# A gated cross-attention block on one core: the maxima of a group of heads half a group further ahead

## What is computed

```
q = rms_norm(x @ w_q.T + b_q, g_q); k, v and k_img, v_img likewise from the context
img_x = softmax(q @ k_img.T * SCALE) @ v_img
txt_x = softmax(where(mask, q @ k.T * SCALE, -1e9)) @ v
out = (txt_x + img_x) @ w_o.T + b_o
x = x + tanh(g_xattn) * out
x = x + tanh(g_ffn) * ffn(layernorm(x))
```

## Time and profile before

| | |
|---|---|
| median of 3 runs | 3852.16 us (3851.76 to 3853.89) |
| the profiled execution: time | 3848.66 us |
| the profiled execution: span | 3846.9 us |
| TensorE busy | 3264.6 us (85%) |
| VectorE busy | 2226.5 us (58%) |
| ScalarE busy | 1561.6 us (41%) |
| GpSimd busy | 1199.9 us (31%) |
| granted TensorE clock, mean share | 0.902 |

### The profile page before, as it was taken

One profiled execution on the slowest core, in us unless ns is written; L12 is line 12 of the kernel. 1 busy time (PEld: TensorE's weight loads), 2 busy tenths in 40 slices (PEclk: granted clock), 3 DMA queues, 4 the chain that ended last, 5 costly groups with the idle time before them and its releaser, 6 DMA issues. The chain is left out here.

```text
span 3846.9 us, 51052 instructions
## 1 busy us (share of the span) xinstructions
PE 3264.6 (85%) x16256; PEld 1969.7 (51%) x16256; DVE 2226.5 (58%) x3716; ACT 1561.6 (41%) x2933; POOL 1199.9 (31%) x386
## 2 busy tenths in 40 slices
PE   6999999977999899999989999998985551799993
PEld 5777888753343443434344343434423440677773
DVE  5666666645565655656565565656535658433335
ACT  3444343322555555555555555555551110122222
POOL 0000000002575655657565565657560000000000
PEclk8999999986898998989899898989897875899997
DMA  5666667685324242333424243332204542101004
GB/s 148 168 167 166 165 168 167 165 120 123 79 59 94 48 93 56 85 75 65 91 50 94 50 91 70 71 87 54 59 6 137 162 155 87 69 23 44 22 22 175
DMA packets 395564, 367.89 MB, mean 96 GB/s; under 512 B 41392, under 2 KB 324080, under 8 KB 392824
## 3 DMA queue, kind: packets, MB, share of 16 engines
q1 hardware_dynamic: 352776, 331.99, 36.4%
q10 hardware_dynamic: 42624, 33.56, 2.7%
HBM read 227.54 MB, written 137.92 MB: 95 GB/s over the span
## 5 line engine op out<-in xcount | busy, mean ns | idle before, releaser
L874 ACT ACTIVATE at_probs<-at_st 128x512 f32<-128x512 f32 (+1 forms) x1664 | 944.6, 596 | 841.2 <-PE at_st L740 828.3
L902 DVE TENSOR_REDUCE at_cm<-at_mx 128x2 f32<-128x896 f32 x768 | 820.1, 1089 | 668.3 <-PE at_mx L756 667.5
L721 POOL TENSOR_TENSOR at_added<-at_added,at_probs 128x2048 f32<-128x2048 f32 x192 | 877.7, 4572 | 121.3 <-ACT at_probs L874 109.8
L756 PE MATMUL at_mx<-at_kst,at_qst 97*128 97x448 f32 (+1 forms) x2048 | 643.3, 368 | 158.9 <-DVE at_cm L902 115.0
L740 PE MATMUL at_st<-at_qst,at_kst 101*128 101x512 f32 (+1 forms) x1664 | 741.4, 461 | 12.6 <-ACT at_probs L874 12.2
L740 PEld LDWEIGHTS at_st<-at_qst,at_kst 101*128 101x128 f32 (+1 forms) x1664 | 314.1, 194 | 563.7 <-ACT at_probs L874 367.5
L756 PEld LDWEIGHTS at_mx<-at_kst,at_qst 97*128 97x128 f32 x2048 | 391.0, 194 | 287.2 <-DVE at_cm L902 196.2
L778 PE MATMUL at_acc<-at_probs,at_vt 128*32 128x512 f32 (+2 forms) x3584 | 529.8, 668 | 0.0
L721 POOL TENSOR_TENSOR at_added<-at_probs 128x2048 f32<-128x2048 f32 x32 | 146.0, 4562 | 705.8 <-ACT at_probs L874 705.8
L691 POOL MEMSET at_ones<- 128x32 f32 x1 | 0.1, 129 | 826.5 <-POOLq L262 826.5
L1309 ACT ACTIVATE ff_h<-ff_psa,ff_b1c,alpha 128x512 f32<-128x512 f32 x128 | 99.6, 779 | 378.2 <-PE ff_psa L1291 378.2
(11 more groups left out here) (190 smaller groups left out, 4789.3 us busy)
## 6 DMA issues: line engine op xcount, KB each, us to landing
at_kst<-k_high SPq DMA_DIRECT2D x256, 200.1 KB
at_kst<-k_low SPq DMA_DIRECT2D x128, 200.1 KB
pj_xin<-in_ctx_dram SPq DMA_DIRECT2D x96, 256.0 KB, 4.2
k_high<-pj_kh SPq DMA_DIRECT2D x96, 256.0 KB, 3.1
k_low<-pj_kl SPq DMA_DIRECT2D x96, 256.0 KB, 4.7
values<-pj_vs SPq DMA_DIRECT2D x96, 256.0 KB, 4.6
at_vt<-values SPq DMA_DIRECT2D x32, 768.0 KB
at_qst<-q_high SPq DMA_DIRECT2D x64, 256.0 KB, 4.2
```

The costliest lines, as they stand in the source:

```text
L721: pool.tensor_tensor(added[:], so_far, probs[:, SLOT[t]], ALU.add).then_inc(S["add_done"], 1)
L756: pe.matmul(mx[:, bank, 0:kn], qst[w.j][0:MROWS, h, qt * P:(qt + 1) * P], kst[w.j][0:MROWS, h, k0:k0 + kn], start=True, stop=True).then_in ...
L874: act.activation(probs[0:kn, SLOT[t], h, :], st[0:kn, h % 2, :], ACT.Exp, scale=SCALE).then_inc(S["exp_done"], 1)
L902: dve.tensor_reduce(dst, mx[:, 2 * slot:2 * slot + 2, 0:kn], AX.X, ALU.max).then_inc(S["mx_free"], 1)
```

## The change

The maxima of a group are issued in two parts. `EARLY` = 14 of the 32 pairs are issued two groups ahead, in tiles 8 to 12, and the other 18 one group ahead, in tiles 0 to 6. The tops stand in tile 7 (`TOPS`), behind heads 2 and 3. A tile has five places, one behind each of heads 0, 1 and 2 and two behind head 3, and `spread` deals the matmuls over them. Ahead of the first group 14 pairs of the second one are issued. GpSimd's join stands ahead of the third add (`JOIN_AT` = 2). VectorE's body has 18 reductions, the negation, the finish, and 14 reductions of the group after next. The sets of instructions are the same, and ScalarE's copies move with the tops.

```diff
--- before.py
+++ after.py
@@ -564,14 +564,13 @@
         self.G = 3 * i + j
         self.known = isinstance(i, int)
         self.first = self.known and self.G == 0
-        self.last = self.known and self.G == GROUPS - 1
 
     def at(self, step):
         j = self.j + step
         return Group(self.i + (j // 3), j % 3)
 
-    def below(self, n):
-        return self.known and self.G < n
+    def followed(self, step):
+        return not self.known or self.G + step < GROUPS
 
 
 def attend(nc, scratch, out_t, b_v, b_v_img):
@@ -593,7 +592,9 @@
     SUMS_LATE = {(0, 1): [4], (1, 1): [5, 6]}
     TEXT = [0, 1, 2, 3, 4, 7, 8, 9]
     NADD = len(TEXT) - 1
-    JOIN_AT = 4
+    JOIN_AT = 2
+    EARLY = 14
+    TOPS = 7
     RING = 5
     SLOT = [0, 1, 2, 3, 4, 0, 1, 2, 0, 1, 2, 3, 4]
     TRIPLES = GROUPS // 3
@@ -627,10 +628,16 @@
         NC = 2 + 1 + 6
 
         plan = {}
-        places = [(t, h) for t in range(KT) for h in (0, 1, 2, 3, 3, 3)]
-        for n in range(2 * NPAIR):
-            plan.setdefault(places[n], []).append((n // 2, n % 2))
-        top_at = {(11, 1): 0, (11, 3): 1}
+
+        def spread(tiles, heads, step, pairs):
+            places = [(t, h) for t in tiles for h in heads]
+            singles = [(step, m, r) for m in pairs for r in range(2)]
+            for n, single in enumerate(singles):
+                plan.setdefault(places[n * len(places) // len(singles)], []).append(single)
+
+        spread(range(TOPS), (0, 1, 2, 3, 3), 1, range(EARLY, NPAIR))
+        spread(range(TOPS + 1, KT), (0, 1, 2, 3, 3), 2, range(EARLY))
+        top_at = {(TOPS, 2): 0, (TOPS, 3): 1}
 
         def keys(t):
             return P if t < KT - 1 else KLAST
@@ -795,16 +802,15 @@
                 done.then_inc(S["s_done"], 1)
 
             def body(g):
-                w = None if g.last else g.at(1)
                 before = None if g.first else g.at(-1)
                 for t in range(KT):
                     for h in range(HG):
                         scores(g, t, h)
-                        if w:
-                            for m, r in plan.get((t, h), []):
-                                maxima(w, m, r)
-                            if (t, h) in top_at:
-                                tops(w, top_at[t, h])
+                        for step, m, r in plan.get((t, h), []):
+                            if g.followed(step):
+                                maxima(g.at(step), m, r)
+                        if (t, h) in top_at and g.followed(1):
+                            tops(g.at(1), top_at[t, h])
                         if h == 1:
                             if t > 0:
                                 values(g, t - 1)
@@ -824,6 +830,9 @@
                     maxima(Group(0, 0), m, r)
             for half in range(2):
                 tops(Group(0, 0), half)
+            for m in range(EARLY):
+                for r in range(2):
+                    maxima(Group(0, 1), m, r)
             groups(pe, body)
             g = Group(TRIPLES, GROUPS - 1 - 3 * TRIPLES)
             pe.wait_ge(S["exp_done"], NST * GROUPS)
@@ -872,7 +881,7 @@
                         if h == 0:
                             ring(g, t)
                         act.activation(probs[0:kn, SLOT[t], h, :], st[0:kn, h % 2, :], ACT.Exp, scale=SCALE).then_inc(S["exp_done"], 1)
-                        if not g.last and (t, h) in top_at:
+                        if g.followed(1) and (t, h) in top_at:
                             copy_top(g.at(1), top_at[t, h])
                         if before:
                             if (t, h) == (0, 0):
@@ -922,12 +931,15 @@
                 dve.tensor_tensor(res[:], part[:, 0, :], part[:, 1, :], ALU.mult).then_inc(S["res_done"], 1)
 
             def body(g):
-                if not g.last:
-                    for m in range(NPAIR):
+                if g.followed(1):
+                    for m in range(EARLY, NPAIR):
                         reduce(g.at(1), m)
                     negate(g.at(1))
                 if not g.first:
                     finish(g.at(-1))
+                if g.followed(2):
+                    for m in range(EARLY):
+                        reduce(g.at(2), m)
 
             dve.memset(neg[:], 1.0).then_inc(S["const_dve"], 1)
             dve.wait_ge(S["const_dve"], 1)
@@ -938,6 +950,8 @@
             for m in range(NPAIR):
                 reduce(Group(0, 0), m)
             negate(Group(0, 0))
+            for m in range(EARLY):
+                reduce(Group(0, 1), m)
             groups(dve, body)
             finish(Group(TRIPLES, GROUPS - 1 - 3 * TRIPLES))
 
```

## The result

| | before | after |
|---|---|---|
| median of 4 runs each | 3851.96 us (3850.92 to 3853.89) | 3981.68 us (3980.64 to 3982.85) |
| ratio, 95% interval | | 1.0336 (1.0318 to 1.0354) |
| profiled execution, its span | 3848.7, 3846.9 us | 3981.9, 3980.1 us |
| period of a group, mean of groups 1 to 29 | 61.5 us | 66.0 us |
| first score of group 0 | 920.12 us | 939.60 us |

The change makes the kernel slower by 3.4%, 130 us. The forecast was 4015 us with a range of 3885 to 4090: direction and mechanism held, and the forecast is 33 us too high.

What follows compares the result with a forecast made beforehand. TensorE was taken to pace the attention stage's 32 groups, 61.4 us each. Groups 1 to 29 (+162), group 0 (-7), group 30 (-8) and the prologue (+16) made +163 on 3852.2: 4015 us, range 3885 to 4090.

Steps and rivals of the forecast that it cites:

- The mechanism: Tiles 7 and 8: the negation and the finish's last two instructions wait for GpSimd's adds; TensorE stands 8.1 us a group.
- the open question of the prediction: Whether the finish's last two instructions wait for GpSimd's adds in every group; the rows held one such case of each.
- The negation's end: Tile 7: the negation ends with GpSimd's fourth add, at +33.75 us; the tops start at +34.05 after 2.3 of waiting.
- The clock's price: TensorE's work at 1.2 GHz costs 0.33 us for each us of it.
- its stretch: After the 8 us stall in tile 8, some 7 us of resumed work at 1.2 GHz, adding 2.3 us a group.
- The sum of a group: Period 47.6 + 17.1 + 2.3 = 67.0 us against 61.4; +5.6 in each of groups 1 to 29, +162 together.
- The smaller terms: Group 0 about -7, group 30 about -8, the prologue's 14 pairs +16; profiled execution 3.5 us below the median.
- The finish slips past: Rival: in tiles 7 and 8 only the negation waits for GpSimd; clock stays 2.4 GHz, period 57.0, 3725 us; chance 0.12.
- One add is met: Rival: the finish's last instruction gets in before the sixth add; 4.2 us less a group, period 62.8, 3895 us; chance 0.14.
- Slow to the end of the group: Rival: clock at 1.2 GHz from the 8 us wait to the group's end, 20 us, 4.3 more; 4140 us; chance 0.06.
- The lower end of the range: 3885 us, set so that the range also holds the case of only one add met, at 3895 us.
- the covered tops: Tops behind tile 7's values and sums, covering VectorE's last reductions; unhindered, a group loses the 3.4 us slow stretch, perhaps 1 waiting.

Runs made afterwards that it cites:

- experiment 1: Changed kernel with the finish's last two instructions moved behind 12 of the 14 early reductions, in tile 12; the reciprocal stays in tile 7: 3708.82 us, 0.9629 of before.
- experiment 2: Changed kernel with GpSimd's fifth and sixth adds cut to 64 of 2048 columns (sums incomplete), VectorE's order untouched: 3722.12 us, one run.
- experiment 9: Changed kernel with only the finish's last instruction (L931) moved to tile 12; the reciprocal and L927 stay in tile 7: 3854.14 us, 1.0006 of before.
- experiment 6: Kernel before with only the first half of the tops moved, from head 1 to head 2 of tile 11: 3727.50 us, 0.9674 of before.
- experiment 8: Kernel of experiment 5 with tile 8's second early pair behind heads 2 and 3, and the prologue's 14 pairs moved into group 0: 3688.58 us, 0.9579 of before.
- experiment 3: Changed kernel with the join back behind the fourth add (JOIN_AT = 4): 3957.02 us, 1.0278 of before.
- experiment 5: Changed kernel with the finish's last two instructions in tile 12 and the join back behind the fourth add: 3678.67 us, 0.9561 of before.

## Why the prediction was right, point by point

**The mechanism held, step by step.** In group 10, from its first score: tile 7 starts at +29.0 (forecast +29.0); GpSimd's fourth add ends at +33.1 (+33.7); the negation starts at +30.6 and ends at +33.2 (+30.8 and +33.75); the tops start at +33.5 (+34.05); the third pair of tile 8 goes out at +47.0 (+47.6), after a gap in TensorE's issue of 8.0 to 8.1 us (8.1). L927 and L931 are long in each of groups 1 to 29, and experiments 1, 2 and 9 show that these lengths are GpSimd's adds and that TensorE's stall is theirs. Whether they hold for every group was the open question of the prediction, which had one row of each.

**The negation's end** was placed 0.57 us too late, because the fourth add's end was. The wait for that end was right: the negation ends 0.04 us after the add in group 10, as in group 4 before. But the second add starts at +14.4 and not +14.8, an add takes 4.57 and not 4.63, and the join 4.9 and not 5.0, so the chain of adds is 0.6 us early by its fourth. TensorE's last score ahead of the tops starts at +31.8 and the tops at +33.5, 1.7 later (forecast 2.3; as idle time the profile has 1.20), and all that hangs on it, the end of the stall too, came 0.6 earlier.

**The clock's price was right, and its stretch too long.** Behind the stall the rest of a group takes 17.28 us at full clock. That is this window of experiment 1, group 10, from the same matmul on (the forecast had 17.1):

```profile
1547.91:1565.19 17.28, 16.11 (x90) 7.36 (x88) 13.20 (x15) 10.21 (x19) 10.56 (x3) 1.00 0.05 16
```

After the change the same stretch takes 19.51, 19.04 and 18.59 us in groups 10, 11 and 12, with 6.6, 5.0 and 3.9 us of work at 1.2 GHz: 0.34 to 0.35 us for each, where the forecast had 0.33. Experiments 6 and 9 have 0.36 and 0.37 in other tiles; groups 1 to 6 of experiment 1 have 0.25, so the price is not one number. The forecast gave 7 us of slow work to every group, though. Group 10 comes near that, and the mean is 5.1, so the clock costs 1.8 us a group and not 2.3. To look at group 10 alone would hide this.

**The sum of a group:** 0.65 less up to the end of the stall (+46.95 in the mean against +47.6), 0.2 more at full clock, 0.5 less for the clock. That is 66.0 against 67.0. As the period before is 61.46 in groups 1 to 29 and not 61.4, the loss is 4.5 a group and not 5.6, and 29 groups of the difference are 31 of the 33 us.

**The smaller terms** nearly cancel. Group 0 gained 8.2 (7), group 30 8.9 (8), and the forecast added 3.5 for the distance of the profiled execution from the median, which the execution after doesn't have. The first score came 19.5 later (16), but the 14 pairs account for 15.5 of it: from the first tops to the first score it is 17.7 us after the change and 2.2 before. The other 4 lie ahead of that. In this execution the attention stage's first maxima start 3.8 us later (880.9 against 877.1), behind stages that the change doesn't touch.

**The rivals.** "The finish slips past" is what experiment 2 builds, at the same place in VectorE's order: 3722.1, one run, against the 3725 given for it; experiment 1, with the finish moved, has 3708.8. "One add is met" is close to experiment 9: 3854.1 against 3895, a period of 61.4 against 62.8. The early negation and the shorter slow stretch are part of that too (there 5.8 us in group 10, not 7). "Slow to the end of the group" did not come: the clock was at 1.00 from 15 us after the stall's start. The lower end of the range was there for the second of these, and no group after the change was of its kind.

**What the prediction missed altogether** is that the 1.44 us pause of the kernel before, and the fall of the clock around it, could be had without the early stream. It named the covered tops as a part of the gain, and experiment 6 has most of it. The early stream with a finish that meets nothing is 19 us better (3708.8), with the join also out of the way 49 (3678.7).

**Left open.** Why the same pause brought the clock down in groups 1 to 6 of experiment 1 and 2 to 6 of experiment 2 (58.0 us a group there) and in no later one up to group 29 (56.4), why the slow work behind the stall is longer in some groups than in others, and tiles 9 and 11 of experiment 8. To let GpSimd do the finish itself, which would take the shared pair out of the matter, was not tried.

## What to carry to other kernels

Before moving an instruction on an in-order engine, list what else moves in time with it though the order stays: here two finish instructions of 1.3 us together grew to 9.2, because their moment fell on GpSimd's adds and the work that covered them shrank from two tiles to one. Put instructions that meet GpSimd's (here those with two SBUF inputs, and the negation's first) where GpSimd is idle, or behind work that nobody waits for; and price such an edit by the end of the other engine's instruction, not by its own length. A price taken from one group can be off by what its neighbours do: compare a few in a row. And look at a short pause at the head of a slow stretch first: to cover 1.4 us with a block that was there anyway was worth 124 us.

## What was not expected of the hardware

- A small instruction waits as long as a large one: the second instruction of the negation, 128x32, takes 0.20 us alone and 1.21 when it meets an instruction of the join (experiments 3 and 5), and the first one, with a single tensor input, takes 0.19 alone and up to 2.71.
- Which of the negation's two instructions waits depends on the moment: in the changed kernel L920 waits for the add and L922 behind it takes 0.20 in each group; in experiment 3 it is the other way in 22 of groups 1 to 29.
- A pause of 1.42 us in the kernel before went with as long a time at 1.2 GHz, 10.2 us, as the stall of 8 us in group 10 after the change. Of the latter 3.7 us fell into the stall, where they cost nothing, so that only 6.6 us of work were slow; of the former 9.8.
